# Three passes over the FFN weights in the second half of the rows become one, and the second layer norm of that half follows each row block's last tile

## The reference

```python
x = _layernorm(x + attention(x, wq, wk, wv, wo), axis=-1)
row_scale = clip(mean(abs(weight), axis=1), 1e-08, None)
binary_weight = sign(weight / row_scale[:, None])
out = einsum('bsi,oi->bso', x, binary_weight) * row_scale * scale_param
x = _layernorm(x + nan_to_num(out), axis=-1)
```

## Time and profile before

| | us |
|---|---|
| median of the timed runs (three: 5509.56, 5512.16, 5787.79) | 5512.16 |
| the profiled execution | 5247.92 |
| its span on the slowest core (core 3) | 5246.4 |
| spans of the eight cores | 5193.0 to 5246.4 |
| mean granted TensorE clock of the cores | 0.916 to 0.923 of full |

### The profile page before, as it was taken

How to read it: one execution, slowest core, us unless ns; L and a number is a source line. 1 busy time by engine, 2 the same in 40 slices (tenths; PEclk the granted TensorE clock), 3 DMA queues, 4 the chain that set the end, 5 groups by cost and what they waited for, 6 DMA issues and landing times.

```text
span 5246.4 us, 68609 instructions; the slowest of 8 cores (5193.0 to 5246.4 us)
## 1 busy us (share of the span) xinstructions
PE 4352.5 (83%) x20496; PEld 2014.9 (38%) x20496; DVE 1232.6 (23%) x2091; ACT 1289.4 (25%) x2433; POOL 429.2 (8%) x740
## 2 busy tenths in 40 slices
PE   2996899999996999999966997899769996754453
PEld 0456744444442333333323443344334443321221
DVE  0320033333331000000001111111334443332323
ACT  0000033333223666666640100000120112000000
POOL 1000033333330000000000000000000000000000
PEclk9898999999998999999988998899779997886776
DMA  9223266666662000000036778578254437657676
GB/s 162 49 51 45 45 121 130 122 130 122 131 123 97 29 33 33 33 33 33 33 77 140 145 149 162 141 145 160 73 205 169 145 123 263 233 208 254 213 261 220
DMA packets 295016, 661.08 MB, mean 126 GB/s; under 512 B 25992, under 2 KB 169480, under 8 KB 281120
## 3 DMA queue, kind: packets, MB, share of 16 engines
q0 software_dynamic: 162560, 411.15, 34.2%
q1 hardware_dynamic: 132128, 245.54, 14.6%
HBM read 648.25 MB, written 176.18 MB: 157 GB/s over the span
## 4 chain that ended last, share of the span: by engine, by line
PE 72%; DMA 18%; DVE 3%; another core or an unknown queue 3%; issue 3%; SPq 1%; ACT 0%; DVEq 0%; POOL 0%; POOLq 0%; ACTq 0%
DMA xct<-xa_scr 9%; PE ps_s L647 8%; PE ps_s L527 7%; PE ps_b L337 5%; PE ps_d L337 5%; PE ps_c L337 5%; PE ps_a L337 5%; PE ps_s L870 4%; PE ps_d L482 4%; PE ps_b L492 4%; DMA yfd<-yf_scr 3%; PE ps_a L492 2%; PE ps_c L482 2%; PE ps_a L647 2%
## 5 line engine op out<-in xcount | busy, mean ns | idle before, releaser
L870 PE MATMUL ps_s<-sgn,y1t 128*128 128x512 bf16 x2048 | 454.7, 383 | 126.7 <-DMA sgn<-sgn_scr 126.7
L647 PE MATMUL ps_s<-wos,attnh 128*128 128x512 bf16 x2048 | 447.2, 379 | 0.0
L527 PE MATMUL ps_s<-qtb,ktb 128*128 128x512 bf16 (+3 forms) x1280 | 388.6, 346 | 66.6 <-DMA qtb<-qt_scr 39.2
L553 ACT ACTIVATE prbp<-ps_s 128x1024 bf16<-128x1024 f32 x384 | 390.2, 1020 | 154.9 <-PE ps_s L527 152.9
L337 PE MATMUL ps_a<-xtb,ws 128*128 128x512 bf16 x1280 | 301.3, 391 | 100.8 <-DMA xtb<-xt 100.8
L905 ACT ACTIVATE sqt<-tyf 128x512 bf16<-128x512 f32 x128 | 80.6, 630 | 1162.5 <-DVE tyf L894 1162.5
L870 PEld LDWEIGHTS ps_s<-sgn,y1t 128*128 128x128 bf16 x2048 | 201.9, 99 | 375.1 <-issue 138.9
L250 ACT ACTIVATE wabs<-wch 128x512 bf16<-128x512 bf16 x256 | 159.0, 621 | 653.2 <-PE ps_s L259 653.2
L664 ACT ACTIVATE sqtb<-xat 128x512 bf16<-128x512 f32 x128 | 80.7, 630 | 941.2 <-DVE xat L653 844.6
L647 PEld LDWEIGHTS ps_s<-wos,attnh 128*128 128x128 bf16 x2048 | 200.1, 98 | 241.9
L337 PE MATMUL ps_b<-xtb,ws 128*128 128x512 bf16 x1280 | 292.4, 388 | 0.0
(11 more groups left out here) (140 smaller groups left out, 4890.4 us busy)
## 6 DMA issues: line engine op xcount, KB each, us to landing
sgn<-sgn_scr POOLq DMA_DIRECT2D x32, 4096.0 KB, 18.6
wos<-wo_s POOLq DMA_DIRECT2D x16, 4096.0 KB, 34.4
ws<-wq_s POOLq DMA_DIRECT2D x32, 1024.0 KB, 9.9
wch<-wf_s POOLq DMA_DIRECT2D x256, 128.0 KB, 4.5
sgn_scr<-sgnc POOLq DMA_DIRECT2D x256, 128.0 KB, 2.3
xnt<-xn SPq DMA_DIRECT2D x128, 256.0 KB, 4.3
xa_scr<-xat SPq DMA_DIRECT2D x128, 256.0 KB, 2.5
xabh<-xa_scr POOLq DMA_DIRECT2D x32, 1024.0 KB, 6.5
```

Source lines behind the costliest of these rows:

```text
L527: t.matmul(o, l, rr, start=True, stop=s1),
L553: s.activation(o, i_, AF.Exp, scale=ISCALE),
L647: t.matmul(o, l, r, start=s0, stop=s1),
L870: t.matmul(o, l, r, start=s0, stop=s1),
```

## The change

In the second half one `emit_c` takes the place of three. It runs all 8 row blocks per slice, carries the 8 D blocks of the first half, one ahead of each slice, as the first pass did, and in the last slice it writes the D block of each row block of the second half right behind that block's tile.

```diff
-    def emit_c(half, gi, sbls, dpops=(), set_war=False):
+    def emit_c(half, gi, sbls, dpops=(), set_war=False, dlast=None):
...
                 tyf_last[idx % 2] = [W(("c", "yfst", sb, osl)), W(("c", "sq2", sb, osl))]
+                if dlast is not None and osl == OSLn - 1:
+                    dlast[sbl]()
...
     emit_b2(1)
-    emit_c(1, 0, list(range(4)), dpops=emit_d(0))
-    emit_c(1, 1, [4, 5], dpops=emit_d(1, (0, 1, 2, 3)))
-    emit_c(1, 2, [6, 7], dpops=emit_d(1, (4, 5)))
-    for fn in emit_d(1, (6, 7)):
-        fn()
+    emit_c(1, 0, list(range(8)), dpops=emit_d(0), dlast=emit_d(1))
```

## The result

| | before | after |
|---|---|---|
| median of the timed runs, us | 5505.62 (10 runs, 5243.68 to 5787.79) | 5083.1 (10 runs, 5067.49 to 5637.92) |
| ratio | 1 | 0.9644, 95% interval 0.9599 to 0.9689 |
| stage from the first D block of the second half to the end of the span, mean of 8 cores, us | 855.8 (842.6 to 867.3) | 702.4 (694.6 to 713.8; 701.5 on die 0, 703.3 on die 1) |

In most of the timed runs of before, in four of the ten of after, and on die 1 (cores 4 to 7) in the profiled execution of after, the four cores of a die ran at a lower granted clock and ended later, so the ratio, which leaves such runs out, and the stage are what to read here, and rows of after are core 1's, the slowest of die 0.

A forecast was written before the change was run, and what follows sets the result against it. Bound taken: VectorE's chain of DMA waits, not bytes. 4427.0 + 54.0 + 403 + 10 + 13.3 + 185 + 3.1 = 5095.4 us of span, 151 less than before; timed 5512 - 151 = 5361, range 5255 to 5450.

The forecast's parts named there:

- slices 1 to 6: Middle slices on VectorE: D block 13.3, first tile 16.7, seven of 5.32, 67.2 us each; 403 us plus 10.
- the eight pairs and the end: Last slice: eight times a tile and its D block, 23.2 us each, 185 us; then 3.1 to the span's end.
- Bound by VectorE's chain of DMA waits, not by bytes: First pass: GpSimd's sign loads wait for VectorE, TensorE for signs; 46.0 us per four tiles, TensorE needs 27.6.
- a second price: Two-block passes: they add a 4 MB load per 13.8 us of matmuls, which cannot be hidden.
- the rule of the Trainium skill: First tile beside signs: by turns per packet about 9 us, seven slices 54 us shorter, 5307 timed; set aside.
- the trace's 16.7 us: First tile behind a D block, its xct issued behind output stores and beside 4 MB of signs; kept in the sum.
- the price of 5 us for stores and signs apart: First two of slices 1 to 6: sign load apart from output stores, 5.2 us extra each, 10 us more.
- A: Rival: second half runs at the first half's rates, slices of 58.7 us; 221 us less, 5291 timed; chance 0.17.
- B: Rival: pieces at upper ends, last-slice D blocks 17.3 us without prefetch; 75 us less, 5437 timed; chance 0.21.
- C: Rival: last slice's pairs 47.5 us, 44 us slower, 5556 timed; against the change from 42 us on; chance 0.04.
- The other signs named beforehand: New profile: 8 sign loads in the second half, 180 to 195 us from last slice's first tile, TensorE finishing near 4900.
- I carry the difference over as it is: Span to timed median: the 151 us saved is subtracted from 5512, giving 5361 us; in proportion it would be 5353.

The follow-up runs named there:

- early xct: Changed kernel with the next tile's xct load issued ahead of this tile's store, in both halves: ratio 0.9388, stage 568.4 us.
- D blocks at the end: Changed kernel with the second half's D blocks behind all tiles, not each behind its own tile: ratio 0.962, stage 693.3 us.

## Why the prediction was right, and where it was not

**The stage.** The forecast was 702.6 us; 702.4 were measured. Its terms against the mean of die 0: the first slice's tiles 54.0 against 54.6; slices 1 to 6 (403 + 10) / 6 = 68.9 each against 67.9; the D block ahead of the last slice 13.3 against 12.9; the eight pairs and the end 188 against 193.9. No term is off by more than 6 us, and the errors cancel; that the total came out within 1 us is luck. One error is a count: six loads of signs are issued after the first two, and they fall into slices 0 to 5; the forecast has one in slice 6 too. Slices 1 to 5 took 69.1 us each, slice 6 took 61.6, where 67.2 was put. The other is the pairs at the end, 6 us dearer than put. What made it work is that every term was a stretch of VectorE's own timeline that held the waits of the new order already.

**What bounds it.** "Bound by VectorE's chain of DMA waits, not by bytes" held: early xct took 134 us out with the same bytes. The two-block passes had a second price, as stated. The runs put it more simply: a sign load costs some 9 us in both orders, as long as xct is issued late. With xct early in the one pass it costs nothing in the middle slices, since slices 1 to 5 take TensorE's 55.3 us.

**Signs and xct.** In the prediction the rule of the Trainium skill ("DMA: Bandwidth & Descriptors", "Queues, rings and completion order"), that a DMA engine serves the queues that have work in turn, a packet at a time, was read as half the engines' time for each queue, and set aside on the trace's 16.7 us. That reading was too quick. Turns need not be of equal bytes: a row of signs has 32 KB and a row of xct 2 KB, so if turns go by rows or by whole loads, most of the time goes to the signs. Cutting the signs took the longest tile from 16.0 to 11.8 us, which fits the taking of turns; whether a turn is a row or a load, no run shows. The value kept in the sum was the measured 16.7, and it served, partly by luck: 8 of the 20 slices 1 to 5 on die 0 (five on each of four cores) have stores and signs on the first tile, which then took 19.5 us on average, and the other twelve have a first tile of 7.3 and a later one of 15.6. A slice of the first kind took 70.6 us, where 67.2 was put, and one of the second 68.2, where 72.4 was put: the price of 5 us for stores and signs apart did not show.

**The rivals.** A (slices of 58.7 us) fell: a slice held both output stores and signs, as the argument against it had it, and slices 1 to 5 took 69.1 us. With early xct slices do come every 55 us, but from another cause, the earlier issue, and not from A's lower traffic. B fell on prefetch: D blocks behind a tile took 12.8 us and not 17.3; the 17.3 appeared only where no tile stands between them, with D blocks at the end. C was far off: a pair took 23.7 us on die 0, and 42 was its point. The other signs named beforehand came too: eight loads of signs in the second half, 193.9 us from the first tile of the last slice to the end, and TensorE done at 4858 to 4889 on die 0.

**What was wrong: the level, and the size in per cent.** The step "The median of the timed runs lies 264 us above it, and no row tells why ... so I carry the difference over as it is: 5512 - 151 = 5361 us" failed. 5083.1 us was measured, below the range's 5255. The 264 us was no fixed part of a timed run (the sentence in the section on the result says what it was). The spans of the profiled execution were the right base: 5095.4 forecast, 5048.3 to 5084.9 on die 0. On core 1, the slowest of them, the stage was 11 us longer than forecast and began 22 us earlier than the 4392.77 of the sum. In per cent the forecast was 2.7 to 2.9 less. The ratio says 3.6 (3.1 to 4.0), the stage in the profiles 153.4 / 5246 = 2.9. Up to the stage nothing changed: it starts at 4343 to 4393 us before and at 4350 to 4373 on die 0 after. Part of the rest, some 30 us or 0.7%, is the ratio itself: it sets the mean of six times of after (5067 to 5088) against that of only three of before, 5243.68, 5254.79 and 5291.39, and without the last of these it would be 0.967, or 3.3%. What is left is open.

## What to carry to other kernels

Price a new order from stretches of the engine that holds the loop up, waits included, and take the price of each stretch from a place where the same things stand ahead of it. When a whole operand is loaded again for a few row blocks, ask what the load costs the small transfers beside it and not only whether it can be hidden. A load that has a free buffer but stands in its engine's list behind a store that waits for a result is not prefetched: moving one call gained 118 us in the kernel before, where the change, with two thirds of the sign loads gone, gained 153.

## What the runs showed of the hardware

A small load beside a large one in another queue can be held up for about as long as the large one takes. The median of the xct loads (256 KB) from 4384 to 4860 us on core 2 is 2.9 us to landing and that of the loads of signs (4 MB) 14.9, and VectorE waited 14.9 us for an xct issued beside signs (core 1, in the section on the result). Cut into eight, the signs hold one xct up for less time, but the sum over a slice stays nearly the same (54.8 and 52.8 us). Here is the cut's effect on the packets of GpSimd's queue, 4384 to 4860 us on core 2, changed kernel first, signs in eight second:

```profile
q0 software_dynamic: 5283, 43.10, 25.0%
```

```profile
q0 software_dynamic: 11318, 41.25, 26.0%
```

The packets doubled for about the same bytes (43.10 and 41.25 MB), and the share of the engines' time stayed.

The price of loading an operand again was nearly the same in both orders, 9.1 and 9.3 us per 4 MB load on average, although TensorE's waits for signs are 306 us in the one and 9.8 in the other. TensorE's waits for the very operand were not the measure of it. VectorE's wait for the small load beside it was: its fall is the whole of the price on core 0 of the kernel before, and 44 of 47 us in the changed one.
